# A selective scan beside an expert feed-forward: B and C by DMA, the product with B on GpSimd, decays and states in PSUM

## What is computed

```
x' = in_proj_w @ ctx;  u = silu(causal_conv4(x') + conv_b)
dt_lo, Bm, Cm = split(x_proj_w @ u)              # 8 + 16 + 16 rows
delta = softplus(dt_proj_w @ dt_lo + dt_proj_b)
state = state * exp(delta * A) + (delta * u) * B_t      # for each channel and each of 16 n
y = sum_n state * C_t;  x = x + (y + D * u) * silu(layernorm(x))
flat = layernorm(x)
x = x + sum_shared expert(flat) / 2 + sum_routed gate_e * expert_e(flat)
```

## Time and profile before

| | us |
|---|---|
| runs | 417.89, 421.60, 421.77 |
| median | 421.6 |
| the profiled execution | 418.02 |
| its span in the trace | 416.2 |
| PE busy | 374.5 (90%) |
| DVE busy | 307.5 (74%) |
| ACT busy | 214.8 (52%) |
| POOL busy | 119.2 (29%) |

### The profile page before, as it was taken

The page is one execution under the profiler, slowest core; times in us unless marked ns, Lnnn a source line. Parts: engine busy times, 40 slices in busy tenths (PEclk is TensorE's granted clock), DMA queues, the critical chain, the costliest instruction groups (busy, mean ns, idle before and its releaser), DMA issues.

```text
span 416.2 us, 7115 instructions
## 1 busy us (share of the span) xinstructions
PE 374.5 (90%) x2383; PEld 334.5 (80%) x2383; DVE 307.5 (74%) x527; ACT 214.8 (52%) x478; POOL 119.2 (29%) x88
## 2 busy tenths in 40 slices
PE   4555668579999999989999999999999999999996
PEld 3334456468899998878999988888999989999996
DVE  3499997689899955899899666998995634444443
ACT  3777534456544436546543437555432335666672
POOL 0555442003333300023334000133432003535442
PEclk8659889869999999999999999999999999999999
DMA  7343460034686321546764222576753226767520
GB/s 229 90 139 104 109 220 25 5 127 146 204 225 178 110 63 52 180 136 205 236 187 123 75 71 81 161 205 204 204 179 97 58 71 223 238 192 217 166 72 27
DMA packets 37456, 58.62 MB, mean 141 GB/s; under 512 B 5778, under 2 KB 15284, under 8 KB 37428
## 3 DMA queue, kind: packets, MB, share of 16 engines
q1 hardware_dynamic: 37428, 58.27, 46.6%
HBM read 57.06 MB, written 1.18 MB: 140 GB/s over the span
## 4 chain that ended last, share of the span: by engine, by line
PE 76%; DVE 15%; issue 6%; ACT 1%; DVEq 1%; ACTq 0%
PE acc L491 34%; PE z L510 10%; PE z L511 9%; PE z L512 9%; DVE bu L728 5%; DVE bu L721 3%; PE z L425 2%; PE acc L391 2%; PE bb L406 1%; PE cc L415 1%; PE acc L496 1%; DVE stage L822 1%; PE misc L452 1%; PE cc L440 1%; PE bb L433 1%
## 5 line engine op out<-in xcount | busy, mean ns | idle before, releaser
L643 ACT ACTIVATE z<-z,par 128x256 f32<-128x256 f32 x188 | 76.3, 443 | 137.3 <-PE z L512 137.3
L491 PE MATMUL acc<-stage,w 128*128 128x256 f32 x564 | 134.8, 382 | 0.0
L510 PE MATMUL z<-xh,w1l 128*128 128x256 f32 (+1 forms) x376 | 120.2, 320 | 0.0
L491 PEld LDWEIGHTS acc<-stage,w 128*128 128x128 f32 x564 | 102.8, 191 | 12.2
L873 POOL TENSOR_TENSOR ya<-ya,pr 128x512 f32<-128x512 f32 x42 | 54.9, 1307 | 187.9 <-DVE pr L739 187.9
L512 PE MATMUL z<-xh,w1h 128*128 128x256 f32 (+1 forms) x376 | 107.1, 285 | 0.0
L511 PE MATMUL z<-xl,w1h 128*128 128x256 f32 (+1 forms) x376 | 107.0, 285 | 0.0
L728 DVE TENSOR_TENSOR_SCAN bu<-dA,bu 128x512 f32<-128x512 f32 x64 | 78.7, 1240 | 1.7
L510 PEld LDWEIGHTS z<-xh,w1l 128*128 128x128 f32 x376 | 72.0, 191 | 4.9 <-issue 3.1
L511 PEld LDWEIGHTS z<-xl,w1h 128*128 128x128 f32 x376 | 72.0, 191 | 1.6
L512 PEld LDWEIGHTS z<-xh,w1h 128*128 128x128 f32 x376 | 72.0, 191 | 0.0
(11 more groups left out here) (113 smaller groups left out, 390.6 us busy)
## 6 DMA issues: line engine op xcount, KB each, us to landing
w<-in_w SPq DMA_DIRECT2D x92, 256.0 KB, 3.3
gone<-gates SPq DMA_DIRECT2D x64, 256.0 KB, 3.8
stage<-in_w SPq DMA_DIRECT2D x11, 512.0 KB, 3.6
grem<-gates SPq DMA_DIRECT2D x96, 48.0 KB, 3.1
xr<-in_xr SPq DMA_DIRECT2D x4, 256.0 KB, 4.2
x<-in_xT SPq DMA_DIRECT2D x4, 256.0 KB, 3.9
grem<-gates SPq DMA_DIRECT2D x32, 32.0 KB, 2.7
out<-x SPq DMA_DIRECT2D x4, 256.0 KB, 3.8
```

Of the source, the lines that this page charges most:

```text
L491: mm = pe.matmul(acc[:, k, :], weights, h, start=t + k + n == 0, stop=last, skip_group_check=True)
L510: pe.matmul(z[p % ZB][:, i, :], w1l[:, t, one], xh_, start=k == 0, stop=False)
L643: ins = act.activation(z[p % ZB][:, i, :], z[p % ZB][:, i, :], ACT.Relu, bias=b1[:, t:t + 1])
```

## The change

- B and C no longer pass TensorE. ScalarE copies all 40 rows of `x_dbl` to `xd`, SyncE spills the 32 rows of B and C to HBM (`spill_bc`) and loads each chunk's two rows of B and of C, broadcast over the partitions, into rings `bt` and `ct` of four chunks (`load_bc`, two DMAs of 256 KB for each chunk). The steps `B`, `C` and `split` are gone.
- `bu` is computed on GpSimd, one unit ahead of its scan, into a ring of four buffers.
- The decays are written to PSUM, one bank for each k; the scan writes the states over them. Each decay step writes a zero column first. `decay(c, k)` now waits for `prod(c-1, k)`, since the product reads the states there.
- In the head each scan is followed by its product. `stage` moves from `hg`'s memory to `grem`'s and has three slots; the w1 pieces are placed anew, four `w1l` pieces and two `w1h` pieces now beside pairs 1 and 2, the loads of the last two pieces behind the first gate loads; the wait at L640 is gone, and SyncE waits for all pieces ahead of the first `grem` load instead.
- `turn` of batch 0 moves from pair 0 to behind pair 2.

```diff
+WRING = 3
+BRING = 4
+BURING = 4
+UNITS = [(("bu", _c, _k), max(2 * _c + _k - 1, 0)) for _c in range(NC) for _k in range(KD)]
 for _c in range(NC):
-    UNITS += [(("B", _c), 2 * _c), (("C", _c), 2 * _c + 1)]
     for _k in range(KD):
         _u = 2 * _c + _k
-        UNITS += [(("decay", _c, _k), max(_u - 1, 0)), (("bu", _c, _k), _u), (("scan", _c, _k), _u),
+        UNITS += [(("decay", _c, _k), max(_u - 1, 0)), (("scan", _c, _k), _u),
                   (("prod", _c, _k), _u), (("fold", _c, _k), _u)]
...
+HEAD += [(("bu", 0, _k), 0) for _k in range(KD)]
 for _c in range(NC):
-    HEAD += [(("B", _c), 0)]
-    HEAD += [(("decay", _c, _k), 0) for _k in range(KD)] + [(("bu", _c, _k), 0) for _k in range(KD)]
+    HEAD += [(("decay", _c, _k), 0) for _k in range(KD)]
+    HEAD += [(("bu", _c + 1, _k), 0) for _k in range(KD)] if _c + 1 < NC else []
+    HEAD += [("w1l", 0)] if _c in (0, 2, 4, 6, 7) else []
+    HEAD += [("w1h", 0)] if _c in (1, 3, 5, 6) else []
     HEAD += [(n, 0) for n in (("stats",), ("rs1", "nb1"), ("zz",), ("ez1",), ("ez2",), ("ez3",), ("zmul",), ())[_c]]
     HEAD += [("xin", 1), ("cv0", 1)] if _c == NC - 1 else []
-    HEAD += [(("scan", _c, _k), 0) for _k in range(KD)]
-    HEAD += [(("C", _c), 0)] + [(("prod", _c, _k), 0) for _k in range(KD)] + [(("piece", _c), 0)]
+    for _k in range(KD):
+        HEAD += [(("scan", _c, _k), 0), (("prod", _c, _k), 0)]
     HEAD += [(("sum", _c - 1), 0)] if _c else []
...
-OPEN = [[("gates", 0), ("turn", 0)],
-        [(n, 1) for n in (("B", 0), ("C", 0), ("decay", 0, 0), ("decay", 0, 1), ("bu", 0, 0), ("scan", 0, 0), ("prod", 0, 0))],
-        [(n, 1) for n in (("decay", 1, 0), ("bu", 0, 1), ("scan", 0, 1), ("prod", 0, 1), ("B", 1), ("bu", 1, 0),
-                          ("decay", 1, 1), ("scan", 1, 0), ("prod", 1, 0), ("fold", 1, 0), "stats")]]
+OPEN = [[("gates", 0), (("bu", 0, 0), 1), (("bu", 0, 1), 1)],
+        [(n, 1) for n in (("decay", 0, 0), ("decay", 0, 1), ("bu", 1, 0), "w1l", ("scan", 0, 0), ("prod", 0, 0), ("scan", 0, 1),
+                          ("prod", 0, 1))],
+        [("turn", 0)] + [(n, 1) for n in (("bu", 1, 1), ("decay", 1, 0), "w1l", ("decay", 1, 1), ("scan", 1, 0), ("prod", 1, 0),
+                                          ("fold", 1, 0), "stats", "w1h", "w1l", "w1h", "w1l")]]
...
+        bu = sb("bu", [P, BURING, 2 * L])
+        hg = sb("hg", [P, 4, 2, L])
+        stage = grem[:].rearrange("p t l -> p (t l)").rearrange("p (s m) -> p s m", s=WRING)
+        dA = [ps(f"dA{k}", [P, 2, L]) for k in range(KD)]
+        xdt = dA[0]
...
+            def spill_bc(b):
+                eng.wait_ge(S["dtl_done"], b + 1)
+                eng.dma_start(bc_d[b % 2], xd[0:NBC, :]).then_inc(S["bc_spilled"], 16)
+
+            def load_bc(b, c):
+                if b * NC + c >= BRING:
+                    eng.wait_ge(S["prod_done"], (b * NC + c - BRING + 1) * KD)
+                else:
+                    eng.wait_ge(S["bc_spilled"], 16)
+                if c == 0:
+                    eng.wait_ge(S["bc_spilled"], 16 * b + 16)
+                for row, dst, ld in ((2 * c, bt, ld_b), (NS + 2 * c, ct, ld_c)):
+                    eng.dma_start(dst[:, c % BRING], bc_d[b % 2, row:row + 2, :].rearrange(
+                        "(o n) l -> o n l", o=1).broadcast_to([P, 2, L])).then_inc(ld[c % BRING], 16)
...
+            spill_bc(0)
+            load_bc(0, 0)
+            load_bc(0, 1)
+            load_w1(3)
+            load_bc(0, 2)
+            load_bc(0, 3)
+            load_w1(4)
+            load_w1(5)
+            load_bc(0, 4)
+            load_bc(0, 5)
+            load_w1(6)
+            load_bc(0, 6)
+            load_w1(7)
+            load_bc(0, 7)
...
+                    if b == 0 and p == 0:
+                        load_w1(10)
+                        load_bc(1, 2)
+                        load_w1(11)
+                    if b == 0 and p == 1:
+                        load_bc(1, 3)
+                    if 0 < b < B - 1 and p < BRING - 1:
+                        load_bc(b + 1, p + 1)
+                    if b < B - 1 and p in (4, 6, 8, 10):
+                        load_bc(b + 1, BRING + (p - 4) // 2)
+                    if b + 2 < B and p == NP - 2:
+                        spill_bc(b + 2)
+                    if b + 2 < B and p == NP - 1:
+                        load_bc(b + 2, 0)
+                    if b == 0 and p == 4:
+                        eng.wait_ge(w1l_done, NW)
...
 # ScalarE, decay
-                        act.wait_ge(S["scan_done"], (b * NC + c - 1) * KD + k + 1)
+                        act.wait_ge(S["prod_done"], (b * NC + c - 1) * KD + k + 1)
+                    act.activation(dA[k][:, :, 0:1], zeros, ACT.Copy)
                     for j in range(2):
                         n = k * NS + 2 * c + j
-                        ins = act.activation(dA[:, k, j * L + 1:(j + 1) * L], delta[:, k, 1:L], ACT.Exp,
+                        ins = act.activation(dA[k][:, j, 1:L], delta[:, k, 1:L], ACT.Exp,
...
 # VectorE, scan and product
-                    dve.tensor_tensor_scan(bu[:, k, :], dA[:, k, :], bu[:, k, :], 0.0, ALU.mult,
+                    dve.tensor_tensor_scan(flat(dA[k]), flat(dA[k]), bu[:, (c * KD + k) % BURING, :], 0.0, ALU.mult,
                                            ALU.add).then_inc(S["scan_done"], 1)
-                    dve.tensor_tensor(products(b, c)[:, k, :], bu[:, k, :], cc[:].rearrange("p a b -> p (a b)"),
+                    dve.tensor_tensor(products(b, c)[:, k, :], flat(dA[k]), flat(ct[:, c % BRING]),
...
 # GpSimd
+                elif name[0] == "bu":
+                    if c * KD + k >= BURING or not first(b):
+                        pool.wait_ge(S["scan_done"], (b * NC + c) * KD + k + 1 - BURING)
+                    wait_bc(pool, ld_b, b, c)
+                    pool.tensor_tensor(bu[:, r, :].rearrange("p (j l) -> p j l", j=2), bt[:, c % BRING],
+                                       du[:, k:k + 1, :].broadcast_to([P, 2, L]), ALU.mult).then_inc(S["bu_done"], 1)
```

More of the change, by code:

```diff
@@ L70 @@
 NEXT = [("xin", 14), ("cv0", 15), ("taps", 16), ("econv", 17), ("uclip", 17), ("usig", 18), ("u", 19), ("xall", 20),
-        ("dtl", 21), ("split", 21), ("dt", 21), ("sp", 22), ("delta", 23)]
+        ("dtl", 21), ("dt", 21), ("sp", 22), ("delta", 23)]
 BEHIND = ("mean", "logits", "xall", "dt", "turn")
@@ L128, in xattn_ffn_kernel @@
         w2 = sb("w2", [P, RING, 2, DX])
+        with nc.sbuf_tensor("bt", [P, BRING, 2, L], F32) as bt, nc.sbuf_tensor("ct", [P, BRING, 2, L], F32) as ct:
+            pass
         w2l = sb("w2l", [P, 4, 2, DX], F32R)
@@ L341, in gate_rem @@
                     eng.dma_start(grem[at:at + n, t, :], gates_d[b % 2, e:e + 1, :].broadcast_to([n, L])).then_inc(ld_rem, 16)
-            load_xr(1)
+            for i in range(3):
+                load_w1(i)
+            eng.dma_start(ctxT[:, 1], ctx_d[:, 1]).then_inc(ld_ctx, 16)
+            spill_bc(0)
[12 more added lines that the diff above has]
+            load_bc(0, 7)
+            for p in range(RING):
+                load_w2(p)
+            load_xr(1)
+            load_w1(8)
+            load_w1(9)
+            spill_bc(1)
+            load_bc(1, 0)
+            load_bc(1, 1)
             for b in range(B):
@@ L376, in _ @@
             eng.wait_ge(S["stored"], 16 * (B + 1))
-        def xin(b):
-            return bb if type(b) is int and b < 2 else misc
         @block.tensor
@@ L638, in pair @@
             def pair(b, p, beside):
-                if first(b) and p < SKEW:
-                    act.wait_ge(w1l_done, NW)
                 act.wait_ge(S["z_ready"], b * NP + p + 1)
@@ L863, in step @@
             def step(name, b):
-                if name[0] == "piece":
-                    pool.wait_ge(S["scan_done"], (name[1] + 1) * KD)
+                if name == "w1l":
                     split_w1(1)
+                elif name == "gates" and first(b):
+                    pool.wait_ge(S["g34_done"], 1)
+                elif name[0] == "bu":
+                    c, k = name[1:]
+                    r = (c * KD + k) % BURING
+                    if c == 0:
+                        pool.wait_ge(S["delta_done"], b + 1)
+                    if c * KD + k >= BURING or not first(b):
[3 more added lines that the diff above has]
+                                       du[:, k:k + 1, :].broadcast_to([P, 2, L]), ALU.mult).then_inc(S["bu_done"], 1)
                 elif name[0] == "fold":
@@ L878, in step @@
                                            ALU.add).then_inc(S["y_folded"], 1)
-                elif first(b) and name in ("usig", "dtl", "sp"):
-                    split_w1(1)
-                elif name == "rest":
-                    split_w1(len(todo))
             def pair(b, p, beside):
@@ L964 @@
     out = nc.dram_tensor("out_0", (P, KD, B, L), F32, kind="ExternalOutput").ap()
+    bc = nc.dram_tensor("bc", (2, 2 * NS, L), F32).ap()
     gates = nc.dram_tensor("gates", (2, NR, L), F32).ap()
```

(2 more changed lines are left out.)

153 lines of the change are left out of this document (52 added, 101 removed).

## The result

Of four runs the changed kernel's median is 408.1 us (406.21 to 412.22), the kernel before on the same chip 421.5 (417.89 to 421.77): ratio 0.973 with a 95% interval of 0.968 to 0.978. It is faster by 13.4 us, less than half of what the forecast of 393.0 meant, and it lies outside the forecast's range, which ended at 404. The two profiled executions differ by 418.02 - 406.21 = 11.8 us, where the sum said 25.5.

What follows compares the result with a forecast made beforehand. VectorE bounds the head, TensorE's waits for gates and VectorE the opening, TensorE the rest. Gains 4.7 + 7.6 + 2.2 + 7.7 + 3.3 = 25.5 off 418.0 give 392.5, stated as 393; range 386 to 404.

Steps and rivals of the forecast that it cites:

- The head: Head, 20 to 60 us, bound by VectorE: units shrink to 1.94 us, taps at 54.85 instead of 59.55, gain 4.7.
- The working for ScalarE in odd chunks: Head: ScalarE's decays with w1 piece and z-gate step come 0.2 us late, three times, 0.6 in all.
- The opening: Opening of batch 0: second layer of pair 3 at 94.7 instead of 102.33, after the last w1 load; gain 7.6 us.
- B and C out of TensorE: Steady loop: pairs without B or C steps take 3.15 us; gains 2.2 in batch 0, 7.7 in batches 1 and 2.
- the one under DMA: Pairs 4 to 11: DMA share 1.03, backlog about 1 us, covered by gate and w2 loads issued three pairs ahead.
- the boundaries: Boundaries to batches 2 and 3: the 1.83 and 1.50 us that TensorE lacks go too, gain 3.3.
- The one on DMA: Rival: broadcasts collide with gate, w2 and w1 loads; 402, or 406 if boundary stalls also stay; chance 0.08.
- dry rings: Part of the DMA rival, chance 0.08: rings run dry, 2.3 us in each of three stretches, 3 in the head.
- GpSimd did not set the pace: Rival in head and opening: GpSimd or the w1 pieces set the pace, costing 4 and 3 us: 400; chance 0.12.
- The port: Rival, loop and head: scan and GpSimd exclude each other, 3.85 us a pair; 449, slower than before; chance 0.03.
- The move of `turn`: Opening: TensorE does z of pairs 1 and 2 in its former 4.41 us idle time ahead of the gates' transpose.
- Two rivals: GpSimd or w1 pieces in head and opening: 400, chance 0.12; DMA, rings dry in the loop too: 402, chance 0.08.

Runs made afterwards that it cites:

- e4: Changed kernel with the small z-gate step nb1 one chunk later in the head's list: 405.0 us, ratio 0.964 to the kernel before.
- e3: Changed kernel with the last two w1 loads ahead of the gate loads and one low piece moved into the head: 401.8 us, ratio 0.960 to before.
- e7: Changed kernel with e1, e4 and e3 together, e3's moved piece held back until xl of batch 0 is done: 393.4 us, ratio 0.936 to before.
- e2: Changed kernel with B and C loads filling 64 of 128 partitions, a constant elsewhere (leaves work out): 403.0 us, ratio 0.964 to before.
- e9: Changed kernel with e1's grouped gate loads and e2's halved B and C loads together (leaves work out): 404.0 us, ratio 0.964 to before.
- e1: Changed kernel with a batch's 40 small grem gate loads issued as 10, same bytes: 403.3 us, ratio 0.963 to before.
- e5: Changed kernel with decays and states back in SBUF, so scan and product have two SBUF inputs: 478.4 us, ratio 1.138 to before.
- e6: Changed kernel with the transpose of batch 0's gates behind pair 0 again, as before the change: 406.5 us, ratio 0.967 to before.

## Why the prediction was half right, point by point

**The head: right, with one stall not seen, and partly by luck.** Forecast 4.7, measured 4.4 (2.8 and 3.6 in the other two profiles of the changed kernel). The pitch of 1.94, the costs out of PSUM and GpSimd's 1.3 all held. The 4.4 hides three errors: the first scan came 0.7 us earlier than said, from there to the taps it took 34.5 us instead of 32.8, and from the taps to the first z 0.7 less than before, where no change was said. The working for ScalarE in odd chunks, "1.2 + 1.05 + 0.6 + 1.2 = 4.05 against VectorE's chunk of 3.88, 0.2 late", looked only at when decays are ready. It missed that in chunk 1 VectorE itself has a step, `nb1`, ahead of its scan, that needs ScalarE's `rs` at the end of that row: 2.43 us, of which `e4` gets back 1.4 to 2.4.

**The opening: the mechanism named, its price mis-sized.** Forecast 7.6, measured 2.3. The step was "at 354 GB/s (the best 2 us of the loop) 7.4 us, plus 1.7 of latency: 91.7 to 92". Without the head's 4.7 that is 87.0 to 87.3. The last piece's data was there at 91.08. First, the gates' spill took from 76.40 to 79.37, 1.5 us longer than before the change (81.50 to 82.99; why is open), so the loads began at 79.37 instead of 77.9. Then it took 11.7 us to the last piece instead of 9.1, for two reasons. From 81 to 91 us the engines moved 302 GB/s on average, not 354 (though 343 in its last 4 us). And 354 GB/s were set against the 2.6 MB up to the last piece alone (2.5, as that piece has 384 KB), while in the 11.7 us the engines moved 270 GB/s x 11.7 us = 3.2 MB: what SyncE had issued behind that piece shared them before it had landed. So the second layer of pair 3 came at 93.5, where 94.7 - 4.7 = 90.0 was said. Last, nothing in the sum stood for what a stall does to the clock: eight matmuls at 3.78 us instead of 1.89, which is the other 1.9 us up to pair 4. `e3` removes the wait and `e7` shows the opening better than forecast: pair 3 at 86.85.

**B and C out of TensorE: the pitch right, the gain lost in batches 0 and 1.** 3.16 from pair to pair where nothing is late, against the forecast's 3.15. The step that failed is the one under DMA: the queues full, "with a backlog of about 1 us at the end of each such stretch, covered by gate and w2 loads issued three pairs ahead". The share was about right (1.03; measured 0.96). The cover was not there: VectorE waited 19.4 us for gate loads, and TensorE for w2 loads too. What the step left out is SyncE. Each DMA occupies it for 0.47 us, and this stood in the trace of before too. Timeline of SyncE's queue there, one pair from `gone` to the next `gone`:

```profile
109.34 0.43 SPq L336 DMA_DIRECT2D gone<-gates  x1
109.82 1.82 SPq L341 DMA_DIRECT2D grem<-gates  x4
111.68 0.42 SPq L318 DMA_DIRECT2D w<-in_w  x1
112.14 0.43 SPq L336 DMA_DIRECT2D gone<-gates  x1
```

That is 2.8 us of a pair's 3.15 to 3.39, nearly all. The change adds two in every second pair, and the mean becomes 3.3 us for a pair of 3.16. With the DMA engines at 0.96 beside it the landing in the loop of batch 0 goes from 3.9 to 7.2 us (median, up to 9.4), which is more than the ring of four covers. For this part and the boundaries together 13.2 us were forecast and 5.8 came; with the bytes of B and C halved (`e2`, `e9`) 12.4 come, so the gain itself was rightly reckoned where the queue does not hold it. Batch 2 gave nearly all of its share; why it doesn't stall at the same 0.96 was not tried (its `gone` loads land after 6.1 us instead of 7.0 to 7.2), and in the changed kernel's third profile it stalls a little, 0.4 and 0.6 us.

**The boundaries: right, with a new stall beside them.** TensorE has 40.00 of 40 us in 160 to 200, 1.83 more than before. But shortly before each of the first two boundaries a stall of 1.8 to 2.0 us came in, at the norm, as VectorE arrives there late from its waits on `gone`. `e2` and `e9` remove it, `e1` leaves 0.44 and 1.35 us of it.

**The rivals.** The one on DMA (402, with a chance of 0.08) is what happened, in its form "dry rings", and larger than priced. GpSimd did not set the pace: VectorE waited for it 7.1 us in four places, none of them ahead of a wait of TensorE in the loop. The port was rightly weighed: `e5` shows that it is real and dearer than the 449 of the rival, and that two inputs in SBUF is the condition. The move of `turn` was credited with the 4.41 us of idle time; `e6` shows that nothing of it arrives as long as the weight pieces hold pair 3.

**The range** ended at 404 and missed 408.1. Two rivals with the same cause, a full queue in the opening and in the loop, had been given prices one by one; they come together.

## What to carry to other kernels

Count a queue twice: its bytes at the rate that the loop sustains, with what is issued behind the load that matters, and its instructions at the issuing engine's own pace. Here both were near their limit, at 0.47 us for each DMA and a share of 0.96, and relief on either side gave 6 us: fewer, larger DMAs of the same bytes, or half of the new bytes. When work moves off a busy engine onto transfers, look first at which loads stand ahead of the one that a pipeline is waiting for. And before GpSimd takes over a product beside VectorE, put one operand of each VectorE operation in PSUM: it was worth 70 us.
